# A gated recurrence in twelve sublayers: fills, solve steps and the output step put in another order, output matrices in two buffers

## The chip, the core and the metric

The kernel runs on one core of a Trainium2 chip. The metric is the device time of one execution in microseconds (us). Before the change it is 2972.5 us, the median of three runs (2965.99 to 2985.49).

## The reference, cut to what matters

Twelve sublayers (cross attention, attention and feed-forward, four times) are added to x one after the other; x is 64 sequences of 32 tokens of 128 numbers. The change touches only the fifth, `L1_attn`, a gated delta rule with two states of 64 x 64 in each of 16 heads:

```python
def step(carry, inp):
    S, R = carry
    q_t, k_t, v_t, a_t, aR_t, b_t, g_t = inp
    kn = k_t / jnp.maximum(jnp.linalg.norm(k_t, axis=-1, keepdims=True), 1e-12)
    pred = jnp.einsum('bhji,bhj->bhi', S, kn)
    r = jnp.clip(v_t - pred, -CLIP, CLIP)
    S = a_t[..., None] * S
    kp = jnp.einsum('bhd,bhde->bhe', kn, S)
    S = S + b_t[..., None, None] * kn[..., None] * (v_t - kp)[..., None, :]
    o = jnp.einsum('bhji,bhj->bhi', S, q_t)
    R = aR_t[..., None] * R
    kpR = jnp.einsum('bhd,bhde->bhe', kn, R)
    R = R + g_t[..., None, None] * kn[..., None] * (r - kpR)[..., None, :]
    o = o + jnp.einsum('bhji,bhj->bhi', R, q_t)
    return ((S, R), o)
out = jnp.moveaxis(os, 0, 1).reshape(Bs, Ts, DI) @ Wo.T   # x + out
```

## The kernel before, in words

The sublayer (`l1_attn`) never steps through time. It takes 128 tokens (four sequences) at a time, in 16 groups. For a group it builds, by halving the 32 steps in five levels, the 32 x 32 matrices that say how much of each earlier step reaches each later one, inverts two of them, and applies matrices to the values. All orders are written out by hand, one list for each engine, and the engines wait for each other by counting semaphores. The lists are loops over i from 0 to 17; in round i three groups are in work: group i has its matrices built ("now"), group i-1 is inverted on GpSimd ("mid"), group i-2 is solved and put out ("old"), and group i+1 has its projections made ("new").

TensorE (`@block.tensor`). `fill_s(i, lv)` and `fill_r(i, lv)` compute the products of keys with weighted rows for levels 1 to 4 of the S and the R state (helper `fill`, L3176; 64 small matmuls each, which the trace has as 128 matmul records, since an f32 matmul is two). `fill_0` is level 0 for both states at once, in two halves j, each behind `row0` of its half. `project_q`, `_k`, `_ar`, `_a` are projections of the next group (L3113), `project_nb` and `broadcast` make the key norms (L3149 to L3152, L3164). The old group goes through `values`, then the solve steps y, z, u, p, y2, z2, wr (all in `apply`, L3213, 64 records each), then `step_o` (L3281, L3282, 128 records) and `step_out` (L3295). A solve step needs the step before it, copied out of PSUM by ScalarE or corrected by VectorE.

VectorE (`@block.vector`). `keep_s` and `keep_r` copy the wanted corners of a fill from PSUM into `ms`, `mr`, `ll` under a mask; `advance_s` and `advance_r` multiply the rows, key columns and running gates for the next level, and wait for the fill of their own level, whose operands they overwrite. `corner` (after z and z2) and `clip` (after p) belong to the old group, `turn` and `turn_back` transpose for GpSimd, `norms` and `keys` belong to the next group's keys, `begin` (two halves, twelve instructions, L3398 to L3400) makes the rows for level 0, and `result` adds a finished group to X.

ScalarE (`@block.scalar`). `take` copies a step's result out of PSUM, `take_gate` applies the sigmoids, `widen(i, j)` spreads the five scaled matrices of a group into `wideM` (L3035; j = 1 and 2 are the output matrices), `widen_x` the inverses into `wideX`, `columns` copies the keys. `widen` waits for `scaled`, which GpSimd's `scale(i)` (L2952 to L2956) counts at the end of a group's inversion, and for the step that read the buffer last.

Each list is strict: what stands behind a wait waits too. The end of a round is, on TensorE, wr, `step_o`, `fill_0` of the next group; on VectorE `keep_r(i, 4)`, `begin(i + 1)`, and then `keep_s(i + 1, 0)`, which waits for both halves of `fill_0`.

## Time and profile before

| | us |
|---|---|
| median of three runs | 2972.5 |
| lowest, highest | 2965.99, 2985.49 |
| the profiled execution | 2988.48 |
| its span | 2986.7 |
| TensorE busy in the span | 2402.1 (80%) |
| VectorE busy | 1942.5 (65%) |
| ScalarE busy | 1362.3 (46%) |
| GpSimd busy | 1001.1 (34%) |
| mean granted TensorE clock | 0.89 of full speed |

The numbers are of one profiled execution, which took 16 us more than the median. The recurrence lies between about 880 us and 1946 us of the span, a third of it. The busy shares are averages over twelve sublayers with different limits, so what the change is worth can only be read inside that stretch. "issue" in a wait means that the profile shows nothing that the engine waited for. DMA figures in that stretch are small: no data is loaded there.

### The profile page before, as it was taken

Reading aid. Unit: us, or ns where it says so; the run is one execution under the profiler, and the core shown is the slowest. Engines: PE = TensorE matmul, PEld = TensorE weight load, DVE = VectorE, ACT = ScalarE, POOL = GpSimd, SP = SyncE. Lnnn points to the kernel's source line nnn. Section 1 sums busy time; section 2 is a strip of 40 time slices with the busy share of each in tenths; the row PEclk is TensorE's granted clock in tenths of the full one; section 3 lists DMA queues with packets and bytes.
Section 4 is the critical chain, followed back from the end, with each engine's and each line's share of the span. In section 5 each row is a group of like instructions: output and inputs, shape, how many; then the busy total and the mean of one; then the engine's idle time right before and its main releaser. Section 6 shows DMA issues by size and latency. Waiting matters only on the chain. (4 is left out here: it accounts for less than half of the span.)

```text
span 2986.7 us, 115635 instructions
## 1 busy us (share of the span) xinstructions
PE 2402.1 (80%) x49947; PEld 1863.7 (62%) x49947; DVE 1942.5 (65%) x4625; ACT 1362.3 (46%) x3252; POOL 1001.1 (34%) x1250
## 2 busy tenths in 40 slices
PE   8987478999986688787787886669998997787754
PEld 6755465665555577677776775547776564575633
DVE  3448335777756887777887887257777666564752
ACT  5443133444434344454444543447776553563420
POOL 0000324655550355334553355311111440360004
PEclk9979687999997798998999999969999998897875
DMA  3200331111110000000000000002221003242014
GB/s 101 64 1 29 105 125 53 47 47 46 47 58 2 3 4 4 4 4 4 4 4 4 4 4 4 3 26 62 61 61 61 4 4 108 62 111 67 5 43 122
DMA packets 80270, 117.47 MB, mean 39 GB/s; under 512 B 11490, under 2 KB 66034, under 8 KB 79234
## 3 DMA queue, kind: packets, MB, share of 16 engines
q1 hardware_dynamic: 71250, 100.31, 10.9%
q0 software_dynamic: 8576, 10.53, 1.7%
q8 instruction: 365, 5.98, 0.8%
q14 instruction: 79, 0.65, 0.1%
HBM read 98.16 MB, written 16.51 MB: 38 GB/s over the span
## 5 line engine op out<-in xcount | busy, mean ns | idle before, releaser
L2469 POOL TENSOR_SCALAR l1xs_p<-l1xs_p,l1xs_col 128x257 f32<-128x257 f32 x256 | 234.4, 936 | 204.5 <-DVE l1xs_col L2425 204.5
L3176 PE MATMUL psum<-l1d_rw,l1d_cols 64*32 64x48 f32 x16384 | 191.0, 211 | 111.9 <-issue 86.4
L3176 PEld LDWEIGHTS psum<-l1d_rw,l1d_cols 64*32 64x32 f32 x16384 | 166.3, 109 | 131.3 <-issue 122.6
L2390 ACT ACTIVATE l1xs_p<-psum,l1xs_col 128x257 f32<-128x257 f32 x256 | 119.7, 473 | 209.7 <-DVE l1xs_col L2420 203.6
L2945 POOL TENSOR_TENSOR l1d_kc<-l1d_ms,l1d_beta 128x512 f32<-128x512 f32 x16 | 17.3, 1083 | 493.4 <-DVE l1d_ms L3487 478.1
L3432 DVE TENSOR_TENSOR l1d_rw<-l1d_rw,l1d_tots 128x1536 f32<-128x1536 f32 (+1 forms) x96 | 138.1, 1438 | 65.7 <-PE psum L3176 64.7
L2432 DVE STREAM_TRANSPOSE l1xs_pt<-l1xs_p 128x288 f32<-128x288 f32 x256 | 122.4, 478 | 79.2 <-POOL l1xs_p L2469 79.1
L2977 ACT COPY l1d_ya<-psum 128x512 f32<-128x512 f32 x96 | 54.9, 583 | 222.7 <-PE psum L3213 222.6
L3113 PE MATMUL psum<-XN,l1d_wp 128*128 128x128 f32 x1024 | 143.9, 297 | 10.3 <-issue 8.3
L3113 PEld LDWEIGHTS psum<-XN,l1d_wp 128*128 128x128 f32 x1024 | 131.1, 207 | 23.9 <-issue 20.9
L2354 PE MATMUL psum<-l1xs_pt,l1xs_vals 32*128 32x512 f32 x1152 | 136.6, 604 | 0.0
L2342 PE MATMUL psum<-l1xs_keys,l1xs_qx 128*32 128x257 f32 x2048 | 132.9, 392 | 3.7 <-DVE l1xs_qx L2414 1.9
L2634 PE MATMUL psum<-consts,l2x_p 128*86 128x128 f32 x768 | 118.5, 277 | 0.8 <-ACT l2x_pt L2693 0.5
L1986 POOL TENSOR_TENSOR l2a_phi<-l2a_pos,l2a_ex 128x512 f32<-128x512 f32 x64 | 80.0, 1272 | 116.3 <-ACT l2a_ex L1972 116.3
L2719 ACT ACTIVATE l2x_p<-psum,l2x_top 128x257 f32<-128x257 f32 x256 | 117.9, 475 | 0.2 <-DVE l2x_top L2757 0.2
L2580 POOL TENSOR_TENSOR l2x_lane<-l2x_rec,l2x_pick 128x128 f32<-128x128 f32 x64 | 25.7, 401 | 234.6 <-DVE l2x_rec L2764 129.9
L3213 PE MATMUL psum<-l1d_ya,l1d_wideX 64*64 64x64 f32 x2048 | 89.3, 256 | 17.9 <-issue 10.5
L2420 DVE TENSOR_REDUCE l1xs_col<-psum 128x1 f32<-128x257 f32 x256 | 101.0, 408 | 2.9 <-PE psum L2342 2.6
L2693 DVE COPY l2x_pt<-psum 86x384 f32<-86x384 f32 x128 | 70.8, 553 | 46.5 <-PE psum L2634 36.8
L3213 PEld LDWEIGHTS psum<-l1d_ya,l1d_wideX 64*64 64x64 f32 x2048 | 83.2, 169 | 23.8 <-issue 14.4
L3213 PE MATMUL psum<-l1d_ya,l1d_wideM 64*64 64x64 f32 x2048 | 74.7, 230 | 28.4 <-ACT l1d_a L3007 13.1
L2323 PEld LDWEIGHTS psum<-XN,l1x_wqk 128*128 128x128 f32 x512 | 66.7, 204 | 47.0 <-issue 32.6
(563 smaller groups left out, 6775.9 us busy)
## 6 DMA issues: line engine op xcount, KB each, us to landing
l2f_w<-in_l2f_w SPq DMA_DIRECT2D x16, 768.0 KB
l1xs_vals<-in_ctx_strips SPq DMA_DIRECT2D x16, 576.0 KB
l0f_w<-in_l0f_w SPq DMA_DIRECT2D x15, 579.0 KB
l0x_ctxT<-in_ctxT SPq DMA_DIRECT2D x16, 516.0 KB, 3.8
l1xs_keys<-in_ctxT SPq DMA_DIRECT2D x16, 516.0 KB
l2x_ctxK<-in_ctxT SPq DMA_DIRECT2D x64, 129.0 KB, 2.1
l2x_ctxV<-in_ctxT SPq DMA_DIRECT2D x64, 129.0 KB, 2.1
l3f_w<-in_l3f_w SPq DMA_DIRECT2D x15, 193.5 KB
```

The costliest lines, as they stand in the source:

```text
L2342: mm = nc.tensor.matmul(score_ps(t)[32 * c:32 * c + 32, :S2], qx[:, g % 2, n, 32 * c:32 * c + 32], keys[:, g % 2, c, :S2], start=True, sto ...
L2354: mm = nc.tensor.matmul(u_ps[c][:], vals[r, g % 2, j, :], pt[r, g % 2, :, j, :], start=(j == 0), stop=(j == STRIP - 1))
L2390: nc.scalar.activation(p[:, t % 4, :S2], score_ps(t)[:, :S2], ACT.Exp, bias=col[:, 0, t % 4:t % 4 + 1], accum_out=col[:, 1, t % 4:t % 4 + ...
L2420: nc.vector.tensor_reduce(col[:, 0, t % 4:t % 4 + 1], score_ps(t)[:, :S2], AX.X, ALU.max, negate=True).then_inc(s["mx"], 1)
L2432: nc.vector.transpose(pt[:, g % 2, n].rearrange("p j r -> p (j r)"), p[:, t % 4, :]).then_inc(s["pt"], 1)
L2469: nc.gpsimd.tensor_scalar(p[:, t % 4, :S2], p[:, t % 4, :S2], col[:, 2, t % 4:t % 4 + 1], None, ALU.mult).then_inc(s["norm"], 1)
L2634: mm = nc.tensor.transpose(t_ps[j % 2][:KC, c * 128:(c + 1) * 128], p[:, l, j, c * KC:(c + 1) * KC], k.const("ident"))
L2719: nc.scalar.activation(p[:, l % 2, j, :S2], s_ps[j][:, :S2], ACT.Exp, bias=top[:, l % 2, j:j + 1], accum_out=sums[:, l % 2, j:j + 1]).then ...
L3113: mm = nc.tensor.matmul(k.ps[into + j][:, e * 128:(e + 1) * 128], wp[:, n, c:c + 128], tokens(i), start=True, stop=True)
L3176: mm = nc.tensor.matmul(k.ps[bank0 + pr + e // per * 2][b * T:b * T + T, e % per * w:(e % per + 1) * w], columns[rr, at:at + T], moving[rr ...
L3213: mm = nc.tensor.matmul(k.ps[bank(name) + h // 8][rr, (h % 8) * 64:(h % 8 + 1) * 64], lhs(h)[rr], rhs[rr, h * 64:(h + 1) * 64], start=base ...
L3432: tt(x, x, over, ALU.mult)
```

## The change

What it does, part by part:

1. Output matrices in two buffers. `widen` with j = 1 and 2 writes, for odd groups, into a second tile `wideN`, which is the memory of the layer norm's row buffer (cleared by GpSimd once the norm's columns are read). Those two calls then wait for the `step_o` of the group before the last instead of the last one, and `step_o` reads `output(i, j)`.
2. `fill_0` (both halves) stands ahead of `step_o` on TensorE, and `step_out` of a group moves from the end of its round to the start of the next, behind `values`.
3. Fills, projections and solve steps alternate in another order on TensorE: `project_q` comes behind `fill_s(i, 1)`, `fill_r` of each level stands earlier against the solve steps, `broadcast` comes behind `fill_r(i, 4)`.
4. VectorE: `result` behind `advance_s(i, 0)`; the first `corner` behind `keep_r(i, 1)`; `clip` behind `keep_r(i, 2)`; the second `corner` behind `keep_s(i, 4)`; `keep_r(i, 4)` ahead of `turn_back` and `keys`.
5. ScalarE: all four `widen` calls of group i-1 stand ahead of the copy of wr, and the copy of o comes last, behind `columns` and `widen_x`.

No work is added or removed but for one memset.

```diff
+        wideN = norm.bufs[5][:].rearrange("p c j d -> p (c j d)").rearrange("p (n h t) -> p n h t", n=2, h=H)
+        output = lambda i, j: wideM[:, j] if i % 2 == 0 else wideN[:, j - 1]
...
+            pool.wait_ge(norm.s["cols"], NCH)
+            nc.gpsimd.memset(wideN, 0.0).then_inc(s["zero"], 1)
...
-                if i > 0:
-                    act.wait_ge(s[needs], i * 2)
+                ahead = 1 if j in (1, 2) else 0
+                if i > ahead:
+                    act.wait_ge(s[needs], (i - ahead) * 2)
+                to = output(i, j) if ahead else wideM[:, j]
...
-                if old:
-                    take(i - 2, "wr_mm", ya, "A", "wr")
                 if mid:
                     widen(i - 1, 3)
                     widen(i - 1, 0)
-                if old:
-                    take(i - 2, "o_mm", rd, "B", "o")
-                if mid:
                     widen(i - 1, 1)
                     widen(i - 1, 2)
+                if old:
+                    take(i - 2, "wr_mm", ya, "A", "wr")
                 if new:
                     columns(i + 1)
                 if mid:
                     widen_x(i - 1, 0)
+                if old:
+                    take(i - 2, "o_mm", rd, "B", "o")
...
                 if old:
                     step_wr(i - 2)
-                if old:
-                    step_o(i - 2)
                 if new:
                     fill_0(i + 1, 0)
                     fill_0(i + 1, 1)
                 if old:
+                    step_o(i - 2)
+                if i >= NT:
                     step_out(i - 2)
...
-                if old:
-                    clip(i - 2)
-                if now:
                     keep_s(i, 2)
                     advance_r(i, 2)
                     keep_r(i, 2)
+                if old:
+                    clip(i - 2)
...
+                    keep_s(i, 4)
                 if old:
                     corner(i - 2, "z2_mm", rd, "t2")
                 if now:
-                    keep_s(i, 4)
+                    keep_r(i, 4)
+                if mid:
+                    turn_back(i - 1)
                 if new:
                     keys(i + 1)
-                if mid:
-                    turn_back(i - 1)
-                if now:
-                    keep_r(i, 4)
```

**The end of a full round on TensorE.** Before (z2, `fill_s` of level 4, `broadcast`, `fill_r` of level 4, wr, `step_o`, then, after 60 more of its matmuls in turn, `fill_0` and the next round's first steps):

```order
L3213 MATMUL psum<-l1d_ya,l1d_wideM 64x64 x32
L3176 MATMUL psum<-l1d_rw,l1d_cols 32x48 x64
L3164 MATMUL psum<-l1d_small,l1d_hsel 128x128 x8
L3176 MATMUL psum<-l1d_rw,l1d_cols 32x32 x64
L3213 MATMUL psum<-l1d_ya,l1d_wideX 64x64 x32
L3281 MATMUL psum<-l1d_wideM,l1d_u 64x64
L3282 MATMUL psum<-l1d_wideM,l1d_ya 64x64
...
L3176 MATMUL psum<-l1d_rw 32x112 x64
L3295 MATMUL psum<-l1d_rd,l1d_wo 128x128 x8
L3226 MATMUL psum<-l1d_wv,XN 128x512 x2
```

Now (the lines are numbered five higher; an odd group, whose output matrices lie in the norm's buffer):

```order
L3181 MATMUL psum<-l1d_rw,l1d_cols 32x48 x64
L3218 MATMUL psum<-l1d_ya,l1d_wideM 64x64 x32
L3181 MATMUL psum<-l1d_rw,l1d_cols 32x32 x64
L3169 MATMUL psum<-l1d_small,l1d_hsel 128x128 x8
L3218 MATMUL psum<-l1d_ya,l1d_wideX 64x64 x32
L3181 MATMUL psum<-l1d_rw 32x112 x64
L3286 MATMUL psum<-ln_xn,l1d_u 64x64
L3287 MATMUL psum<-ln_xn,l1d_ya 64x64
```

`fill_0` has passed `step_o`, and `fill_r` of level 4 has passed the broadcasts.

**The end of a full round on VectorE.** Before (second `corner`, `keep_s` of level 4, `keys`, `turn_back`, `keep_r` of level 4, the first instruction of `begin`):

```order
L3534 TENSOR_TENSOR l1d_ya<-psum,l1d_rd 128x512 x2
L3493 COPY_PREDICATED l1d_ll<-l1d_lmask,psum 128x256
L3494 COPY_PREDICATED l1d_ms<-l1d_lmask,psum 128x16x16
L3495 COPY_PREDICATED l1d_ms<-l1d_lmask,psum 128x16x16
L3385 TENSOR_TENSOR l1d_rw<-psum,l1d_cols 128x512 x2
L3528 STREAM_TRANSPOSE l1d_kc<-l1d_xi 128x1024
L3514 COPY_PREDICATED l1d_mr<-l1d_lmask,psum 128x16x16
L3515 COPY_PREDICATED l1d_ll<-l1d_lmask,psum 128x256
L3398 TENSOR_TENSOR l1d_rw<-l1d_rw,l1d_a 128x512
```

Now (the lines are numbered seven higher):

```order
L3500 COPY_PREDICATED l1d_ll<-l1d_lmask,psum 128x256
L3501 COPY_PREDICATED l1d_ms<-l1d_lmask,psum 128x16x16
L3502 COPY_PREDICATED l1d_ms<-l1d_lmask,psum 128x16x16
L3541 TENSOR_TENSOR l1d_ya<-psum,l1d_rd 128x512 x2
L3521 COPY_PREDICATED l1d_mr<-l1d_lmask,psum 128x16x16
L3522 COPY_PREDICATED l1d_ll<-l1d_lmask,psum 128x256
L3535 STREAM_TRANSPOSE l1d_kc<-l1d_xi 128x1024
L3392 TENSOR_TENSOR l1d_rw<-psum,l1d_cols 128x512 x2
L3405 TENSOR_TENSOR l1d_rw<-l1d_rw,l1d_a 128x512
```

The transpose back and the two multiplications of `keys` now stand between `keep_r` of level 4 and `begin`.

**The end of a full round on ScalarE.** Before (the copy of wr, `widen` 3 and 0, the copy of o, `widen` 1 and 2, `columns`, `widen_x`, the copy of the next values):

```order
L2977 COPY l1d_ya<-psum 128x512 x2
L3035 ACTIVATE l1d_wideM<-l1d_ll,l1d_part 128x16x16 x2
L3035 ACTIVATE l1d_wideM<-l1d_ms,l1d_part 128x16x32 x2
L2977 COPY l1d_rd<-psum 128x512 x2
L3035 ACTIVATE l1d_wideM<-l1d_ms,l1d_part 128x16x32 x2
L3035 ACTIVATE l1d_wideM<-l1d_mr,l1d_part 128x16x32 x2
L3052 COPY l1d_cols<-l1d_rw 128x1024
L3055 COPY l1d_cols<-l1d_rw 128x1024
L3045 ACTIVATE l1d_wideX<-l1d_kc,l1d_part 128x16x32 x2
L2977 COPY l1d_v<-psum 128x512 x2
```

Now (an even group; `widen` 0 and 1 show as one row):

```order
L3041 ACTIVATE l1d_wideM<-l1d_ll,l1d_part 128x16x16 x2
L3041 ACTIVATE l1d_wideM<-l1d_ms,l1d_part 128x16x32 x4
L3041 ACTIVATE l1d_wideM<-l1d_mr,l1d_part 128x16x32 x2
L2981 COPY l1d_ya<-psum 128x512 x2
L3058 COPY l1d_cols<-l1d_rw 128x1024
L3061 COPY l1d_cols<-l1d_rw 128x1024
L3051 ACTIVATE l1d_wideX<-l1d_kc,l1d_part 128x16x32 x2
L2981 COPY l1d_rd<-psum 128x512 x2
L2981 COPY l1d_v<-psum 128x512 x2
```

The copy of wr, for which `step_o` waits, now stands behind four `widen` calls that wait for GpSimd.

## Rows read from the trace of the kernel before

**Rows 1.** The page, costliest groups: TensorE's fills, busy, mean ns, idle before.

```profile
L3176 PE MATMUL psum<-l1d_rw,l1d_cols 64*32 64x48 f32 x16384 | 191.0, 211 | 111.9 <-issue 86.4
```

**Rows 2.** The timeline of VectorE: start, duration; first keep of rounds 2 and 15.

```profile
1028.51 1.32 DVE L3465 COPY_PREDICATED l1d_ms<-l1d_imask,psum 128x128 f32<-128x128 int32 x4 [1.91 <-PE psum L3176]
...
1821.48 1.32 DVE L3465 COPY_PREDICATED l1d_ms<-l1d_imask,psum 128x128 f32<-128x128 int32 x4 [4.89 <-PE psum L3176]
```

**Rows 3.** Waits, 1148 to 1822 us, 11 rounds: total, times, longest.

```profile
DVE l1d_ms L3465 <- PE psum L3176: 57.4, 12, 6.0
...
PE psum L3176 <- DVE l1d_tots L3437: 10.9, 11, 1.2
PE psum L3213 <- ACT l1d_a L3007: 10.7, 9, 1.7
```

**Rows 4.** The timeline of TensorE in round 15, a stretch full of fills.

```profile
1852.51 1.41 PE L3176 MATMUL psum<-l1d_rw,l1d_cols 64*32 64x48 f32 x127 [0.93 <-issue]
1856.09 1.32 PE L3176 MATMUL psum<-l1d_rw,l1d_cols 64*32 64x32 f32 x124 [2.17 <-issue]
```

**Rows 5.** Windows there: length, engines' busy us, TensorE clock, DMA share, GB/s.

```profile
1849.60:1850.00 0.40, 0.40 (x22) 0.40 (x18) 0.40 (x1) 0.00 (x0) 0.40 (x1) 1.00 0.19 41
...
1853.60:1854.00 0.40, 0.31 (x28) 0.20 (x15) 0.13 (x1) 0.00 (x0) 0.40 (x1) 1.00 0.17 41
```

**Rows 6.** The timeline of TensorE, start of round 8 and the wr before it.

```profile
1387.56 3.68 PE L3213 MATMUL psum<-l1d_ya,l1d_wideX 64*64 64x64 f32 x64
...
1397.73 2.05 PE L3295 MATMUL psum<-l1d_rd,l1d_wo 128*128 128x128 f32 x16
1399.62 1.88 PE L3226 MATMUL psum<-l1d_wv,XN 128*128 128x512 f32 x4
1401.68 2.02 PE L3113 MATMUL psum<-XN,l1d_wp 128*128 128x128 f32 x16 [0.18 <-DVE X L3548]
1404.48 2.08 PE L3213 MATMUL psum<-l1d_v,l1d_wideX 64*64 64x64 f32 x64 [0.78 <-ACT l1d_v L2977]
```

**Rows 7.** The timeline of VectorE, end of round 7: keys, transpose, keep, begin.

```profile
1384.51 1.29 DVE L3385 TENSOR_TENSOR l1d_rw<-psum,l1d_cols 128x512 f32<-128x512 f32 x2 [2.48 <-PE psum L3164]
1385.84 1.25 DVE L3528 STREAM_TRANSPOSE l1d_kc<-l1d_xi 128x1024 f32<-128x1024 f32 x1
1387.70 0.44 DVE L3514 COPY_PREDICATED l1d_mr<-l1d_lmask,psum 128x256 f32<-128x256 int32 x1 [0.62 <-PE psum L3176]
...
1393.13 0.42 DVE L3400 TENSOR_TENSOR l1d_rw<-l1d_rw,l1d_ar 128x256 f32<-128x256 f32 x1
...
1398.15 1.33 DVE L3465 COPY_PREDICATED l1d_ms<-l1d_imask,psum 128x128 f32<-128x128 int32 x4 [4.61 <-PE psum L3176]
1401.22 0.31 DVE L3548 TENSOR_TENSOR X<-X,psum 128x128 f32<-128x128 f32 x1
```

**Rows 8.** The timeline of VectorE, end of round 0, which has no output step.

```profile
966.47 0.44 DVE L3514 COPY_PREDICATED l1d_mr<-l1d_lmask,psum 128x256 f32<-128x256 int32 x1 [0.38 <-PE psum L3176]
...
974.22 1.30 DVE L3465 COPY_PREDICATED l1d_ms<-l1d_imask,psum 128x128 f32<-128x128 int32 x4 [1.91 <-PE psum L3176]
```

**Rows 9.** Timelines in round 8: TensorE's broadcasts, and VectorE's clip of one half.

```profile
1443.95 1.16 PE L3164 MATMUL psum<-l1d_small,l1d_hsel 32*128 32x128 f32 x16
...
1424.20 0.69 DVE L3542 TENSOR_TENSOR l1d_rd<-psum,l1d_v 128x512 f32<-128x512 f32 x1 [0.21 <-PE psum L3213]
1424.92 0.43 DVE L3543 TENSOR_SCALAR l1d_rd<-l1d_rd 128x512 f32<-128x512 f32 x1
```

**Rows 10.** The timeline of ScalarE and GpSimd near the end of the sublayer.

```profile
1909.24 0.59 ACT L2977 COPY l1d_ya<-psum 128x512 f32<-128x512 f32 x1 [4.21 <-PE psum L3213]
1910.66 0.91 ACT L3035 ACTIVATE l1d_wideM<-l1d_ll,l1d_part 128x256 f32<-128x256 f32 x2
1911.47 1.32 ACT L3035 ACTIVATE l1d_wideM<-l1d_ms,l1d_part 128x512 f32<-128x512 f32 x2
...
1908.96 1.04 POOL L2956 TENSOR_TENSOR l1d_mr<-l1d_mr,l1d_beta 128x512 f32<-128x512 f32 x1
```

42 lines of the change are left out of this document (22 added, 20 removed).

## The prediction

> **What bounds the kernel now.** The page first: its costliest groups name the fills of the recurrence, where most of TensorE's idle time is not a wait for any engine but "issue" [rows 1]. The timeline of VectorE gives the length of a round there: from the first keep of round 2 to that of round 15 are 792.97 us, 13 rounds of 61.0 us [rows 2]. Only these full rounds, with an old, a middle and a new group, are much touched by the change; nothing outside the sublayer is. Then the waits: VectorE waits for the two halves of `fill_0` at the head of every round, 57.4 us in twelve waits, 4.8 us each, while TensorE's waits for other engines are about 1 us a round apiece (for the first `advance_s`, and for the sigmoids ahead of z2) [rows 3].
>
> What is "issue"? In a stretch full of fills the timeline shows stalls 3.58 us apart, 127 matmul records between them, whatever the step at hand [rows 4]. A record has a weight load beside it, so with the waits that is 256 instructions. The windows show the DMA engines at 41 GB/s for 0.4 us, 4.0 us apart, and no data is loaded there: that is 16 KB of instructions each time [rows 5]. So TensorE's instructions arrive in pages, and a new one each 3.6 to 4.0 us, call it 3.7. I count a round from the code: nine times 128 records of fills, seven solve steps of 64, 128 in `step_o`, 64 in the projections and 56 in the rest, 1848, that is 14.6 pages or 54 us of the 61. A page of fills takes 1.4 us and waits 2.2; where few records take long, the instructions wait instead. A round is therefore held by three things in turn: the pages, the chain through fills and VectorE, and TensorE's own order at the end of a round.
>
> The Trainium skill, "Runtime: NRT & Kernel Launch", section "Instruction fetch mechanics", has the same 16 KiB blocks, but says that TensorE holds 128 KiB of them and that a boundary is "mostly hidden". The trace disagrees: 2.17 us were lost at one boundary [rows 4]. By that rule no reordering could win or lose anything at pages; the sum below would stand, and the lower end of its page term would be void.
>
> **The end of a round.** I start at `keep_r(i, 4)`. Before, it and `begin` take 5.85 us to 1393.55, then VectorE waits 4.8 us, because TensorE still does wr (3.68 us at half speed), the copy, `step_o`, and only then `fill_0` [rows 7, 3, 6]: 10.6 us in the mean. Now `fill_0` passes `step_o`, but the transpose (1.25) and `keys` (1.29) have come between [rows 7]. What `fill_0` then costs can be read off round 0, which has no old group: from `keep_r` to the next keep 7.75 us, 1.9 behind the end of `begin` [rows 8]. So 5.85 + 1.25 + 1.29 + 1.9 = 10.3, a gain of only **0.3**. Four of the five microseconds won by passing `step_o` are spent on work that stood in the shadow of fills and now stands in the open, and on a fill at half clock, since TensorE idles in front of it. At full clock (2.08 for 3.68 in a solve step, [rows 6]) the fill's second half would take 1.1, the gain 1.1. A page boundary in the broadcasts, for which `keys` waits, would add up to 2.2 and turn it into a loss of 1.9.
>
> **The rest of a round,** up to `keep_r(i, 4)`:
> - `result` behind `advance_s(i, 0)`: the first fill may start 0.31 us sooner [rows 7]: **-0.3**, at least where TensorE is there in time.
> - `broadcast` behind `fill_r(i, 4)`: that fill comes 1.16 sooner [rows 9]: **-1.2**. Where pages decide, it is 16 records, an eighth of a page, -0.5.
> - `clip` behind `advance_r(i, 2)` and `keep_r(i, 2)`: `project_nb` waits for it, and y2, the next fill and the sigmoids stand behind. `clip` is twice 0.69 + 0.43, 2.2 us [rows 9], which no longer run while TensorE does `fill_r(i, 2)`. It costs 0 where TensorE is late through pages and 2.2 where it is not; but `fill_s(i, 3)`, some 1.4 us [rows 4], now stands ahead of `project_nb` and covers part: **+1.2**, between the two and nearer what is left uncovered.
> - After `fill_0` at half clock, `step_o`, `values`, `step_out` and y have to be done before the first fill. At the solve step's full rate that is at most 2 x 2.08 + 1.88 + 2.05 + 2.08 = 10.2 us; before, `step_out`, `values`, a projection and y were through 8.8 us after 1397.73, just as VectorE was ready [rows 6]. Half speed adds up to 1.6 to a solve step [rows 6]. Bounds 0 and +2; I take **+0.3**, since the two engines have slack again until the second level.
> - Pages: before, `step_out`, `values` and `project_q` stand together, 2.05 + 1.88 + 2.02 us for 36 records [rows 6], and the pages wait. Now the projection is two fills away. Where pages decide the round this is worth up to 2.0; I take **0**, because what ends a round is now the chain of VectorE, which the pages reach only through the fills. Bounds -2.0 and 0.
> - The second buffer for the output matrices, and the first `corner` behind `keep_r(i, 1)`: nothing. `widen` of 1 and 2 no longer waits for `step_o`, but ScalarE idles for long stretches anyway; u waits some 2 us longer for its corner, and its only follower in the chain, p, comes ahead of a `clip` that is itself later. `turn` keeps its place among the fills, so GpSimd's inversion, which ends after `turn` by the same distance, is not later. The memset of `wideN` on GpSimd lies in the prologue, under the projections.
>
> Sum of a round: -0.3 - 1.2 + 1.2 + 0.3 - 0.3 = **-0.3 us**, in 13 rounds **-4**. The ends: low (-0.3 - 1.2 + 0 + 0 - 2.0 - 1.1) = -4.6, high (0 - 0.5 + 2.2 + 2 + 1.9) = +5.6; neither is likely in every round, since a page boundary falls elsewhere each time.
>
> **The last rounds** lose. With no fills left, wr, its copy and `step_o` are the path. The copy of wr began at 1909.24; GpSimd's scale ended at 1910.00 [rows 10]. Now four `widen` pairs stand ahead of the copy, 0.8 for the narrow and 1.25 for each of three others as they follow each other [rows 10], 4.6 us from 1910.0; the copies of wr end at 1915.7 instead of 1910.8. The copy of o, behind `widen_x`, then starts with the end of `step_o`, and all behind it comes some 4.5 us later. In the round before the same order costs about 1, since its scale was done earlier. Together **+5.5**.
>
> The sum is -4 + 5.5 = +1.5 against the profiled execution's 2988.5, so 2990; that execution lies 16 us above the median of its runs, so I forecast **2974 us**, no change. A measurement of this kernel tells about 1%, 30 us, from no change; its three runs alone span 19.5.
>
> **The rivals.**
> - *Pages decide (F).* If the rounds are held by pages rather than by VectorE, the light projection among fills gives its 2.0, the broadcasts 0.5, the first fill 0.3, and VectorE's chain at the end has time to spare with `fill_0` at full clock, 0.8 + 0.3: -3.9 less about 1 for the clock at the head and a part of `clip`, so -2.9 a round, -38 + 5.5: **2940**. For it: 54 of 61 us. Against: a round before already ends with a wait of VectorE that has no page in it.
> - *The exposed chain (S), slower.* `keys` waits for the broadcasts, and `begin` for `keys`, and TensorE for `begin`: three engines' steps in series that nothing covers, ahead of a fill at half clock. If `clip` costs its full 2.2 (+1.0 on my sum), the head the 1.6 of one step at half speed (+1.3), and one round in four loses 2.2 at the broadcasts (+0.5), a round is 2.5 longer: +33 + 5.5, **3011**. It decides as soon as VectorE's idle time at the keep falls under 2 us while the one for `norms` or the broadcasts grows above 2. For it: round 0, where nothing hides the 1.9 us behind `begin` [rows 8]. Against: the pages give TensorE time at each idle.
>
> By the rule on fetching cited above, F would be void and its chance would go to the forecast and to S.
>
> **Chances.** Forecast 0.66 (own range 2955 to 2998), F 0.20, S 0.14. Of F nearly all is faster by over 1% (under 2943) or at its edge, and a little of the forecast's case; of S most is over 3002. So faster 0.19, same 0.69, slower 0.12. The range goes from 2938, with F's value in it, to 3000.
>
> **What would show each step.** VectorE's idle before the first keep at 2 us in place of 4.8, with 10.3 us from `keep_r(i, 4)` to the keep; `fill_0` in two pieces with a gap, the clock at half there; `keep_r(i, 4)` some 50 us behind the first keep, as now (61.0 - 10.6 = 50.4); "issue" still 7 to 9 us a round; in the last rounds `widen` ahead of the copy of wr and 5 us more. Wrong would be a round under 59.5 (F) or over 62.5 (S), or a `widen` wait in full rounds that holds `step_o`.

## The result, and the profile after

The changed kernel takes **3030.9 us** (median of four, 3024.61 to 3059.54) against 2972.5: a ratio of **1.021**, 95% interval 1.0136 to 1.0283, so slower by about 2%. The profiled execution of it took 3024.61 us with a span of 3022.8. It is the fastest of its four, and the profiled execution of the kernel before, 2988.48, was slower than all of its timed runs, so the two profiles differ by 36 us and the medians by 58. What is read from them below explains the 36; the other 22 are not in these two traces.

VectorE's timeline gives the rounds, first keep of round 2 and of round 15, as in [rows 2]:

```profile
1028.31 1.32 DVE L3472 COPY_PREDICATED l1d_ms<-l1d_imask,psum 128x128 f32<-128x128 int32 x4 [1.91 <-PE psum L3181]
...
1854.89 1.32 DVE L3472 COPY_PREDICATED l1d_ms<-l1d_imask,psum 128x128 f32<-128x128 int32 x4 [1.91 <-PE psum L3181]
```

Everything before round 2 is as it was. Thirteen rounds take 826.58 us, **63.58 each**, in place of 61.00: +33.6 us. The last rounds (first keep of round 15 to the end of the last `step_out`) take 132.8 in place of 124.4: +8.4. The rest of the program, behind the last `step_out`, gives 5.7 back: the span grew by 36.1.

I cut each round at the first copy of `keep_r(i, 4)`: the **head** runs from the round's first keep to it, the **end** from it to the next first keep. Means of rounds 2 to 14: head 50.5 before and 53.2 after, end 10.5 before and 10.4 after. So the end of the round does what was forecast, and the head does not.

The fills' group of the page, which answers to [rows 1]:

```profile
L3181 PE MATMUL psum<-l1d_rw,l1d_cols 64*32 64x48 f32 x16384 | 187.4, 208 | 93.3 <-issue 68.1
```

TensorE's "issue" at the fills fell, by 18 us in the whole kernel, while the rounds grew. Its named waits grew instead. The waits of 1148 to 1855 us (total, times, longest), beside [rows 3]:

```profile
PE psum L3181 <- DVE l1d_rw L3407: 31.1, 24, 2.8
DVE l1d_small L3382 <- ACT l1d_small L3024: 23.8, 11, 3.6
DVE l1d_ms L3472 <- PE psum L3181: 19.9, 12, 2.3
PE psum L3154 <- DVE l1d_rd L3550: 15.5, 6, 4.8
PE psum L3118 <- ACT l1d_u L2981: 8.5, 11, 0.8
```

The first keep waits 1.7 us a time in place of 4.8: `fill_0` has passed `step_o`. But TensorE now stands before `fill_0` for VectorE's `begin` (first row), VectorE stands before `norms` for ScalarE's root of the key norms, 2.2 us a round (second), TensorE stands before `project_nb` for the clip (fourth), and before `project_ar` for ScalarE's copy of u (fifth). Before, the wait for the clip was 3.4 us in five times, and those for the root and for u were not there.

The end of round 9 on VectorE and TensorE: `keep_r`, transpose, `keys`, the last of `begin`, first keep; and `fill_0` in two pieces at half clock, as in [rows 7, 8]:

```profile
1460.12 0.44 DVE L3521 COPY_PREDICATED l1d_mr<-l1d_lmask,psum 128x256 f32<-128x256 int32 x1 [1.46 <-PE psum L3181]
...
1460.79 1.24 DVE L3535 STREAM_TRANSPOSE l1d_kc<-l1d_xi 128x1024 f32<-128x1024 f32 x1
1461.95 1.25 DVE L3392 TENSOR_TENSOR l1d_rw<-psum,l1d_cols 128x512 f32<-128x512 f32 x2
...
1468.00 0.42 DVE L3407 TENSOR_TENSOR l1d_rw<-l1d_rw,l1d_ar 128x256 f32<-128x256 f32 x1
1470.33 1.03 DVE L3472 COPY_PREDICATED l1d_ms<-l1d_imask,psum 128x128 f32<-128x128 int32 x3 [1.91 <-PE psum L3181]
```

```profile
1466.02 1.75 PE L3181 MATMUL psum<-l1d_rw 64*32 64x112 f32 x64 [2.14 <-DVE l1d_rw L3407]
1468.47 1.75 PE L3181 MATMUL psum<-l1d_rw 64*32 64x112 f32 x64 [0.71 <-DVE l1d_rw L3407]
```

That is 10.2 us. One window over the thirteen rounds, before and then after (length; busy us and instructions of TensorE, its weight loads, VectorE, ScalarE, GpSimd; TensorE's granted clock, DMA share, GB/s):

```profile
1028.00:1822.00 794.00, 634.21 (x24033) 572.88 (x24015) 632.92 (x1028) 376.94 (x741) 361.14 (x507) 0.93 0.02 4
```

```profile
1028.00:1855.00 827.00, 657.25 (x23901) 593.42 (x23894) 660.07 (x1027) 380.01 (x742) 362.20 (x507) 0.89 0.02 4
```

With the same instructions (but for one `step_o`, which now falls behind the end of the window) TensorE is busy 23 us longer, at a granted clock of 0.89 in place of 0.93 (the mean of stretches at 2.4 and at 1.2 GHz), and **VectorE is busy 27 us longer**. For VectorE the rows by form say which instructions (before, then after):

```profile
L3543 DVE TENSOR_SCALAR l1d_rd<-l1d_rd 128x512 f32<-128x512 f32 x26 | 13.4, 516 | 0.9
...
L3440 DVE TENSOR_TENSOR l1d_tots<-l1d_tots 128x256 f32<-128x256 f32 x26 | 11.1, 426 | 0.9
```

```profile
L3550 DVE TENSOR_SCALAR l1d_rd<-l1d_rd 128x512 f32<-128x512 f32 x26 | 21.6, 830 | 0.9
...
L3447 DVE TENSOR_TENSOR l1d_tots<-l1d_tots 128x256 f32<-128x256 f32 x26 | 20.6, 792 | 0.9
```

The clip's bound took 516 ns in the mean and takes 830; the product of the running gates took 426 and takes 792. Both read and write SBUF only. What they meet there, in round 5, VectorE and then GpSimd:

```profile
1236.02 1.18 DVE L3447 TENSOR_TENSOR l1d_tots<-l1d_tots 128x256 f32<-128x256 f32 x1
...
1250.18 0.43 DVE L3550 TENSOR_SCALAR l1d_rd<-l1d_rd 128x512 f32<-128x512 f32 x1
1250.52 0.68 DVE L3549 TENSOR_TENSOR l1d_rd<-psum,l1d_v 128x512 f32<-128x512 f32 x1
1251.24 1.01 DVE L3550 TENSOR_SCALAR l1d_rd<-l1d_rd 128x512 f32<-128x512 f32 x1
```

```profile
1235.87 1.10 POOL L2949 TENSOR_TENSOR l1d_kc<-l1d_ms,l1d_beta 128x512 f32<-128x512 f32 x1 [29.80 <-ACT l1d_wideX L3051]
...
1250.30 3.29 POOL L2925 TENSOR_TENSOR l1d_tmp<-l1d_lt,l1d_xi 128x512 f32<-128x512 f32 x2
```

The same clip instruction takes 0.43 us when it starts 0.12 us ahead of GpSimd's long one and 1.01 when it starts beside it, while the subtraction from PSUM between them keeps its 0.68. The Trainium skill, "SBUF — State Buffer", section "Who interferes with whom", says that one pair of SBUF ports is shared between VectorE and GpSimd and locked, the loser waiting for it. These rows agree.

In round 16, which has no fills any more, ScalarE's four `widen` calls stand ahead of the copy of wr, as forecast [rows 10]:

```profile
1946.48 0.91 ACT L3041 ACTIVATE l1d_wideM<-l1d_ll,l1d_part 128x256 f32<-128x256 f32 x2 [6.70 <-POOL l1d_mr L2960]
1947.29 1.32 ACT L3041 ACTIVATE l1d_wideM<-l1d_ms,l1d_part 128x512 f32<-128x512 f32 x2
1948.52 1.32 ACT L3041 ACTIVATE ln_xn<-l1d_ms,l1d_part 128x512 f32<-128x512 f32 x2
1949.74 1.32 ACT L3041 ACTIVATE ln_xn<-l1d_mr,l1d_part 128x512 f32<-128x512 f32 x2
1950.96 1.04 ACT L2981 COPY l1d_ya<-psum 128x512 f32<-128x512 f32 x2
```

Counted from round 15's first keep the copies end at 97.1 us in place of 89.3. 4.5 of the 7.8 are the `widen` calls. Another 3.0 were there before them: GpSimd's scale ended 91.6 us behind that keep in place of 88.5. The cause is the same order one round earlier, in round 15, which has no new group. There the four `widen` calls waited for GpSimd, the copy of wr behind them, and `step_o` for the copy:

```profile
1903.53 0.91 ACT L3041 ACTIVATE l1d_wideM<-l1d_ll,l1d_part 128x256 f32<-128x256 f32 x2 [14.55 <-POOL l1d_mr L2960]
...
1909.20 0.44 PE L3286 MATMUL psum<-ln_xn,l1d_u 64*64 64x64 f32 x2 [7.03 <-ACT l1d_ya L2981]
```

Before, `step_o` waited 0.78 us there. All behind it came 3 us later, ScalarE's second `widen_x` too, and GpSimd could begin the next inversion only behind that. In the full rounds, where a new group's fills are at hand, the `widen` calls waited for GpSimd as well (13.8 us in six of them), but no wait of `step_o` shows.

### The profile page after: what moved, and what is told of

Its sections match the earlier page's. It is cut to its first block and busy times, and to the rows that moved or that the text cites. A ratio compares the mean times of both kernels' runs of the same rounds, so it can differ in the third digit from the quotient of the medians.

```text
span 3022.8 us, 115597 instructions
## 1 busy us (share of the span) xinstructions
PE 2421.3 (80%) x49925; PEld 1886.7 (62%) x49947; DVE 1967.2 (65%) x4625; ACT 1364.0 (45%) x3252; POOL 1004.7 (33%) x1251
## 3 DMA queue, kind: packets, MB, share of 16 engines
q1 hardware_dynamic: 71250, 100.31, 10.6%
## 5 line engine op out<-in xcount | busy, mean ns | idle before, releaser
L3439 DVE TENSOR_TENSOR l1d_rw<-l1d_rw,l1d_tots 128x1536 f32<-128x1536 f32 (+1 forms) x96 | 137.3, 1430 | 51.2 <-PE psum L3181 50.8
L2342 PE MATMUL psum<-l1xs_keys,l1xs_qx 128*32 128x257 f32 x2048 | 132.8, 392 | 3.5 <-DVE l1xs_qx L2414 1.9
L2693 DVE COPY l2x_pt<-psum 86x384 f32<-86x384 f32 x128 | 70.8, 553 | 49.4 <-PE psum L2634 36.7
L3218 PE MATMUL psum<-l1d_ya,l1d_wideX 64*64 64x64 f32 x2048 | 83.3, 246 | 19.3 <-DVE l1d_ya L3541 13.8
L2342 PEld LDWEIGHTS psum<-l1xs_keys,l1xs_qx 128*32 128x32 f32 x2048 | 61.7, 111 | 53.6 <-issue 24.4
L2354 PEld LDWEIGHTS psum<-l1xs_pt,l1xs_vals 32*128 32x128 f32 x1152 | 54.5, 184 | 62.7 <-issue 62.5
```

What stands on the lines that cost most here:

```text
L2342: mm = nc.tensor.matmul(score_ps(t)[32 * c:32 * c + 32, :S2], qx[:, g % 2, n, 32 * c:32 * c + 32], keys[:, g % 2, c, :S2], start=True, sto ...
L2354: mm = nc.tensor.matmul(u_ps[c][:], vals[r, g % 2, j, :], pt[r, g % 2, :, j, :], start=(j == 0), stop=(j == STRIP - 1))
L3218: mm = nc.tensor.matmul(k.ps[bank(name) + h // 8][rr, (h % 8) * 64:(h % 8 + 1) * 64], lhs(h)[rr], rhs[rr, h * 64:(h + 1) * 64], start=base ...
L3439: tt(x, x, over, ALU.mult)
```

## The experiments

Each ran in one group with runs of the kernel before on the same chip; times are medians, ratios are to the kernel before of that group, with 95% intervals. Round, head, end and last rounds are read from the profiled execution as above, in us. The kernel before had medians of 2972.5 to 2985.2 in the different groups, so a difference of medians between two groups is good to about 10 us, and the ratios are the safer comparison.

| kernel | time | ratio | round | head | end | last |
|---|---|---|---|---|---|---|
| before | 2972.5 | 1 | 61.00 | 50.5 | 10.5 | 124.4 |
| changed | 3030.9 | 1.021 | 63.58 | 53.2 | 10.4 | 132.8 |
| e1 middle alone | 3048.5 | 1.0207 (1.0165 to 1.025) | 65.98 | 56.3 | 9.7 | 124.2 |
| e2 middle put back | 2993.4 | 1.0048 (1.0023 to 1.0073) | 60.70 | 53.4 | 7.3 | 133.3 |
| e3 norms later | 3032.9 | 1.0165 (1.0122 to 1.0207) | 63.46 | 53.0 | 10.5 | 134.9 |
| e4 ScalarE's last rounds | 3030.8 | 1.015 (1.0106 to 1.0193) | 64.34 | 53.9 | 10.4 | 123.1 |
| e5 fewer records | 2940.6 | 0.9838 (0.9791 to 0.9886) | 57.04 | 49.5 | 7.6 | 123.2 |
| e6 less work | 2980.5 | 0.9979 (0.9957 to 1.0) | 60.53 | 49.4 | 11.1 | 126.8 |
| e7 first half back | 3047.6 | 1.021 (1.0158 to 1.0263) | 64.25 | 53.8 | 10.5 | 134.0 |
| e8 second half back | 3011.6 | 1.0103 (1.0057 to 1.0149) | 61.06 | 50.7 | 10.4 | 135.8 |
| e9 queries back too | 2998.9 | 1.0063 (1.0041 to 1.0086) | 61.85 | 54.5 | 7.4 | 132.5 |
| e10 copy of y first | 2962.6 | 0.9956 (0.9935 to 0.9977) | 58.43 | 51.1 | 7.3 | 132.4 |
| e11 e9 and e4 | 2988.2 | 1.003 (1.0012 to 1.0049) | 61.12 | 53.9 | 7.3 | 126.8 |
| e12 e10 and e4 | 2953.1 | **0.9917** (0.9893 to 0.9941) | 58.61 | 51.4 | 7.3 | 126.6 |
| e13 broadcast back | 3052.9 | 1.0251 (1.0222 to 1.0279) | 65.05 | 54.8 | 10.2 | 134.3 |
| e14 clip back | 3014.7 | 1.0103 (1.0072 to 1.0135) | 62.22 | 51.8 | 10.4 | 134.9 |
| e15 levels 3, 4 back | 3055.5 | 1.0274 (1.0239 to 1.0309) | 63.71 | 53.3 | 10.4 | 135.6 |
| e16 end lists into e10 | 3001.4 | 1.0059 (1.0036 to 1.0082) | 60.31 | 50.1 | 10.2 | 135.3 |
| e17 end lists back | 3029.5 | 1.013 (1.0094 to 1.0167) | 63.62 | 56.1 | 7.5 | 138.1 |
| e18 short GpSimd | 3003.8 | 1.0077 (1.0048 to 1.0106) | 61.55 | 51.2 | 10.4 | 120.0 |

### Which part of the change: e1 and e2

e1 is the kernel before with the round's middle alone in the new order: all moves on TensorE between y and `fill_r(i, 4)`, and those of `corner` and `clip` on VectorE. e2 is the changed kernel with that middle put back, and with the end of the round on VectorE (`keys`, `turn_back`) and the broadcast put back as well:

```diff
+                    fill_s(i, 3)
+                if new:
+                    project_nb(i + 1)
...
+                if old:
+                    clip(i - 2)
```

> The kernel before with the middle of a round alone in the new order (TensorE: fill_r ahead of project_k, z, u, p, project_nb as in the change; VectorE: both corners and clip moved back); the end of the round, the first fill behind step_o and ScalarE's list stay as before. Theory M (the loss is made in the middle: u, p and so clip come late, project_nb waits for clip, norms for project_nb): the stretch from the first keep to keep_r of level 4 grows from 50.4 to about 53 us, the end stays 10.6, so a round of 63.5 to 64 and 33 to 40 us more than before, about 3008. Rival T (the loss comes from the ends: transpose and keys exposed, the clock at half at the head of a round): the middle alone changes nothing, 2972 within 10.

> The change with the middle of a round put back: TensorE's order from project_k to fill_r of level 4 as before, corner and clip and the last keeps, keys and transposes of VectorE as before; the first fill stays ahead of step_o, output matrices in two buffers, step_out at the head of the next round, project_q behind the first fill, ScalarE's new list. Theory M: the end falls to 0.8 + 5.05 + 1.9 = 7.8 us since keys and the transpose are under fills again, the stretch before it stays near 50.4 to 51.5; a round of 58.2 to 59.3, so 22 to 36 us less in 13 rounds, 8 given back in the last rounds: 2945 to 2958. Rival T: no better than the kernel before, 2972 or more, since the head of a round runs at half clock and pages are late. Rival F (pages hold the round): 2972 less 5 at most.

The middle alone costs 5.0 us a round, more than was expected, and 2% of the kernel, as much as the whole change; with it put back the round is 2.9 us shorter, a little more than the 2.6 that the change had cost, but 1.4 to 2.5 longer than was expected of e2. VectorE's wait for the root of the norms is in e1 about what it is in the changed kernel (1157 to 1820 us), and it is missing in e2, e8, e10, e14 and e16, which have the clip at its old place:

```profile
DVE l1d_small L3373 <- ACT l1d_small L3020: 24.6, 10, 4.2
```

The end of a round of e2, 7.3 us, shows what passing `step_o` is worth when nothing else is put there.

### Is the wait for norms to be had back, and the last rounds: e3 and e4

```diff
-                if new:
-                    norms(i + 1)
                 if now:
                     advance_r(i, 3)
                     keep_r(i, 3)
+                if new:
+                    norms(i + 1)
```

> The change with one move on VectorE: norms stands behind advance_r and keep_r of level 3 in place of ahead of them. Theory M: VectorE waited 23.8 us in 11 rounds for the norms that project_nb, late behind clip, feeds; 2.2 us a round. Behind the keep this wait is covered, the round gets 1.5 to 2.2 shorter, 20 to 29 us less than the change: 3003 to 3011. Rival: the wait only moves on (the broadcasts are needed 6 us later all the same, and fill_r of level 3 is late itself): within 8 us of the change, 3023 to 3031.

No gain. The wait at `norms` is gone, but VectorE's wait for fills at `advance` is 76.6 us in place of 37.4 (1157 to 1820 us). So the loss is not a mere matter of where `norms` stands in VectorE's list. e4 is the changed kernel with, on ScalarE, the copy of wr ahead of `widen` 3 and the copy of o ahead of `widen` 1, only where there is no next group:

```diff
+                if old and not new:
+                    take(i - 2, "wr_mm", ya, "A", "wr")
                 if mid:
                     widen(i - 1, 3)
```

> The change with ScalarE's list of before in the last rounds alone (where no new group follows): the copy of wr ahead of the widening, the copy of o between the widenings. The last rounds took 132.9 us from the first keep of round 15 to the end of the last step_out, against 124.5 before. Theory: all of the 8.4 is the copies of wr and o behind the widening: back to 125, the time 8 us less than the change's, about 3023. Rival: only the 5.5 of the forecast come back and 3 stay, which come from the middle of round 15: 3025.

The last rounds fell by 9.7 us, more than the 8.4 that they had lost, and GpSimd's scale in them ended at 87.9 us in place of 91.6, which bears out the cause given above. What the kernel gained is not settled: its median is the changed kernel's, its ratio 1.015 for 1.021, inside both intervals, and its full rounds came out 0.76 us longer in the profile, with ScalarE's list there the same. In e11 against e9 and e12 against e10, where the same edit was made, the medians fell by 10.7 and 9.5 us and the last rounds by 5.8.

### Records or work: e5 and e6

e5 leaves out seven of eight heads in the fourth fill of the output matrices; e6 leaves out three of four blocks in the two gate projections.

```diff
-                fill(cols[:, 2], 5, 7, lv, 2, 32, 8).then_inc(s["mR_mm"], 1)
+                fill(cols[:, 2], 5, 7, lv, 2, 32, 8, range(1 if lv == 4 else hp)).then_inc(s["mR_mm"], 1)
```

> The kernel before, with the fourth fill of the output matrices doing one of its eight heads: it leaves out 112 of a round's 1848 TensorE records and 1.05 us of its busy time, and nothing else, so its output is not the reference's. Two theories of what TensorE's unnamed stalls cost. Theory instructions: a round's length goes with the number of records, since a stall comes every 256 of them. The round falls by more than the work, by about 3.2 us (112 of 1848 records of 61.0 us, 3.7), and the kernel by about 50 us, to some 2925. Rival work: the round falls by the busy time alone, about 1 us, and the kernel by about 16 us, to some 2960. Third, chain: the fourth fill of the output matrices is not on the path of a round (step_out of the block stands behind the next round's start), and nothing changes within 5 us.

```diff
-                    for e in range(4):
+                    for e in range(1 if i > 0 and n >= 2 else 4):
```

> The kernel before, with the projections of the keys' and of the values' correction (project_a and project_ar) doing one of their four blocks a half: it leaves out 24 records and 3.0 us of TensorE's busy time a round, and its output is not the reference's. Theory instructions: the round falls by what 24 records are worth, about 0.7 us, and the kernel by about 12 us, to some 2965. Rival work: the head of a round is bound by TensorE's own busy time, the round falls by nearly all of it, about 3 us, and the kernel by about 45 us, to some 2930. The two kernels together tell whether a round of the kernel before is counted in records or in busy time.

e5: 112 records, 1.05 us of work, and the round is 3.96 us shorter. e6: 24 records, 3.0 us of work, and the round is 0.47 us shorter. So a round follows its records more than its work, as [rows 4] had it. Neither number is the price of records alone. In e5 the granted clock of the rounds was 0.95 in place of 0.93 and TensorE's busy time fell by 1.8 us a round and not by 1.05, so some 0.75 us are faster matmuls; wr alone took 2.9 us in the mean in place of 3.5. In e6 the clock was 0.89, and the busy time fell by 11 us and not by 39, so that what it left out was partly given back by slower matmuls. e5 shows one thing more: 3.0 of its 3.96 us lie in the end of the round, 7.6 us with `step_o` still ahead of `fill_0`. So the end was long in the kernel before at least in part because TensorE came to it late.

### Which half of the middle: e7, e8, e14, e15, e13

e7 puts back the first half in the changed kernel (of VectorE's list the first `corner` alone moves, not the clip), e8 the second.

```diff
                 if old:
                     step_u(i - 2)
+                if now:
+                    fill_s(i, 2)
                 if new:
                     project_ar(i + 1)
```

> The changed kernel with the first half of the round's middle put back (TensorE: fill_r 1 behind z, fill_s 2 behind u; VectorE: corner and clip of level 1 ahead of advance_r 1), the second half left as changed. Theory spread: the 2.9 us a round that putting back the whole middle gave (63.6 to 60.7) comes from both halves alike, and the round comes to about 62, the kernel to about 3010. Rival first: the wait of project_ar for ScalarE's copy of u is most of it, and the round comes to about 61, the kernel to about 2997. Rival second: the half behind it, with the correction's projection and the clip, is most of it, and the round stays at 63.5 with the kernel at 3030.

```diff
+                if old:
+                    step_p(i - 2)
                 if now:
                     fill_r(i, 2)
-                if old:
-                    step_p(i - 2)
...
-                if now:
-                    fill_s(i, 3)
                 if new:
                     project_nb(i + 1)
```

> The changed kernel with the second half of the round's middle put back (TensorE: project_p ahead of fill_r 2, the next block's projection ahead of fill_s 3, the fills of levels 3 and 4 in the old turn; VectorE: clip ahead of keep_s 2, the second corner ahead of keep_s 4), the first half left as changed. Theory spread: about 62 us a round, the kernel at about 3010. Rival first: the round stays near 63.5 and the kernel at 3030, since the first half is what costs. Rival second: the round comes to about 61 and the kernel to about 2997.

The second half is it: 2.5 us a round and 19 us of the kernel; putting back the first half alone gives nothing or costs a little. e14 puts back the turn of `step_p`, `project_nb` and the clip alone, e15 the turn of levels 3 and 4 alone.

> The changed kernel with project_p ahead of fill_r 2, the next block's norms' projection ahead of fill_s 3 and the clip ahead of keep_s 2 on VectorE; levels 3 and 4 as changed. The whole second half gave 2.5 us a round (63.6 to 61.1). Theory clip: TensorE's wait for the clip ahead of project_nb (15.5 us in eleven rounds, 1.4 each) goes and what follows comes earlier, so this half carries most of it: about 61.5 a round, 3000. Rival corner: the levels 3 and 4 carry it, and this run stays within 0.6 us a round of the changed kernel, 3025.

> The changed kernel with levels 3 and 4 put back: the correction's projection ahead of fill_r 3, z2 ahead of fill_s 4, and on VectorE the second corner ahead of keep_s 4; project_p and the clip as changed. Theory clip: at most 0.6 us a round, about 3025. Rival corner: 2 us a round and more, about 61.3, 2998; the wait of z2 for ScalarE's gate (1.6 us, with z2 at half clock behind it, in the kernels with this order) speaks against it.

The clip's part carries 1.4 of the 2.5 us by the profiled rounds. By the ratios it carries all of it, 1.0103 for e14 and for e8; the profiled execution of e14 was its slowest and that of e8 its fastest, so the 1.1 us between their rounds are not safe. Levels 3 and 4 alone give nothing: the kernel got slower by 25 us with them and the profiled rounds by 0.1. Of the 18 us between the two profiled executions 11 lie ahead of round 2 and 3 in the last rounds; why is not shown. e13 puts back only the broadcast ahead of `fill_r(i, 4)`:

```diff
+                if new:
+                    broadcast(i + 1)
                 if now:
                     fill_r(i, 4)
```

> The changed kernel with the broadcast put back ahead of fill_r 4, nothing else. In all kernels with it ahead and step_o behind fill_0 the end of a round took 7.3 us, in those with it behind 10.4. Theory keys: VectorE's product for the keys then comes before keep_r 4 and off the path, the end of a round falls by 3 us and the head grows by the broadcast's 1.2 or a little more, so a round comes to about 61.9 and the kernel to about 3003. Rival trade: the head grows by as much as the end falls (53.2 to 56.2), nothing changes, 3030.

Wrong, and it shows whose the end of the round is: with `keys` still behind `keep_r(i, 4)` on VectorE the end stays at 10.2, though the broadcast comes sooner, and the head pays 1.6 for it.

### The ends: e9, e10, e16, e17

In e2 TensorE stands before the next projection for ScalarE's copy of y (waits of 1157 to 1820 us):

```profile
PE psum L3118 <- ACT l1d_ya L2981: 20.0, 11, 1.8
```

`project_q` had come behind `fill_s(i, 1)`, and on ScalarE the copy of the queries stands ahead of the copy of y. Both next kernels start from e2: e9 puts `project_q` back ahead of y on TensorE; e10 changes ScalarE's list alone.

```diff
                     step_out(i - 3)
+                if new:
+                    project_q(i + 1)
                 if old and i != NT + 1:
                     step_y(i - 2)
```

> The changed kernel with the middle of the round put back and the next block's query projection put back ahead of step_y as well: of TensorE's lists only step_o behind fill_0 and step_out behind the next round's values are left of the change. In the run with the middle put back, TensorE stood 1.81 us a round behind fill_s 1 for ScalarE's copy of y, which had the copy of the queries ahead of it, and 0.72 ahead of fill_s 1. Theory shadow (step_o costs the head, and the head pays for the order of queries and y): the queries' 2.05 us go under VectorE's work ahead of the first fill, fill_s 1 starts about 1.3 us later, and the 1.8 us wait goes, so that a round falls by about 2.5 us, from 60.7 to 58.2, and the kernel from 2993 to about 2955. Rival pages: the time of a round goes with the number of records alone, which is unchanged, and the kernel stays at about 2993 (60.7 a round).

```diff
+                if old:
+                    take(i - 2, "y_mm", ya, "A", "y")
                 if new:
                     take_q(i + 1)
                 if old:
-                    take(i - 2, "y_mm", ya, "A", "y")
                     widen_x(i - 2, 1)
```

> The changed kernel with the middle put back, the query projection left behind fill_s 1 as changed, and on ScalarE the copy of y ahead of the copy of the queries. Theory shadow: the wait of 1.81 us for the copy of y goes, and with no TensorE work moved the round falls by up to 1.8, from 60.7 to about 59, the kernel to about 2967. Rival pages: nothing, about 2993. Where this one gains and the one with the queries ahead of step_y does not, it was ScalarE's queue; where both gain, the wait behind fill_s 1.

e9 missed, 61.85 us a round for 58.2. Its trace has a new wait of 2.1 us a round: the projection of the queries writes the bank that `result` reads, and `result` now stands behind `advance_s(i, 0)` and `step_out`. No run moved `result`, so how much of the miss it is stays open:

```profile
PE psum L3118 <- DVE X L3555: 21.4, 10, 2.9
```

e10 gained 31 us on e2 by the medians, 2.3 us in each round. It has `step_o` behind `fill_0`, the two buffers and what goes with them (`step_out`, `result` and `project_q` later, ScalarE's new list), and it is 0.4% faster than before: the idea of the change is worth 2.6 us a round (61.00 to 58.43) where the lists around it fit. That is by one profile of each; the medians, 16 us apart with 8 us lost in the last rounds, say nearer 2. The end of one of its rounds, `keep_r`, the last of `begin`, first keep, is VectorE's `begin` and half a fill, with nothing between:

```profile
1426.47 0.40 DVE L3521 COPY_PREDICATED l1d_mr<-l1d_lmask,psum 128x256 f32<-128x256 int32 x1
...
1432.46 0.42 DVE L3407 TENSOR_TENSOR l1d_rw<-l1d_rw,l1d_ar 128x256 f32<-128x256 f32 x1
1434.42 1.04 DVE L3472 COPY_PREDICATED l1d_ms<-l1d_imask,psum 128x128 f32<-128x128 int32 x3 [1.54 <-PE psum L3182]
```

e16 puts the change's end of the round into e10 (broadcast behind `fill_r(i, 4)`, `turn_back` and `keys` behind `keep_r(i, 4)`); e17 takes it out of the changed kernel.

```diff
-                if new:
-                    keys(i + 1)
-                if mid:
-                    turn_back(i - 1)
                 if now:
                     keep_r(i, 4)
+                if mid:
+                    turn_back(i - 1)
+                if new:
+                    keys(i + 1)
```

> The kernel that gained on ScalarE's queue, with the changed order at the end of a round put back in: the broadcast behind fill_r 4, and on VectorE turn_back and keys behind keep_r 4. Theory VectorE: the end of a round is VectorE's own row of work from keep_r 4 on (two copies 0.8 us, four passes of begin 5.2 to 5.9, and now the transpose's 1.25 and the keys' 1.29 as well), so it grows from 7.3 to about 10; the head gives back the broadcast's 1.2 us; a round grows by 1.4, from 58.4 to about 59.8, the kernel from 2963 to about 2985. Rival free: the head gives back 2.7 us, and the kernel stays within 6 us.

> The changed kernel with the broadcast ahead of fill_r 4 and keys and turn_back ahead of keep_r 4, as before. Theory VectorE: the end of a round falls from 10.4 to 7.3 us, the head grows by 1.2 to 1.6 as it did where the broadcast alone was put back (53.2 to 54.8), and a round comes to about 62, the kernel to about 3010. Rival free: head and end trade one for one, 63.6 and 3030.

With the old middle these lists cost 1.9 us a round and 39 us (1.0% by the ratios; 7 us of it ahead of round 2 and 3 in the last rounds of the profile); with the new middle nothing. There what the end saves the head takes. Their price depends on the chain ahead of them.

### The two repairs together: e11 and e12

e11 is e9 and e12 is e10, each with e4's edit.

> The kernel with only step_o, step_out and result moved (queries ahead of step_y, middle as before) and with ScalarE's old list in the last two rounds as well. Its rounds are those of the kernel with the queries ahead of step_y; the last round falls by 8 to 10 us, as it did where ScalarE's old list was put into the changed kernel (132.8 to 123.1 from the first keep of round 15 to the end). Theory: about 2946, below both the kernel before and the changed one by 1% and more. Rival: the last rounds give it back in another place, within 4 us of the run without it.

> The kernel that gained on ScalarE's queue (middle put back, copy of y ahead of the copy of the queries), with ScalarE's old list in the last two rounds as well. The rounds are unchanged at 58.4 us and the last one falls by 6 to 10 (132.4 to 126.8 or 123.1, as in the two runs with the old list): about 2955, some 0.8% below the kernel before. Rival: the last rounds give it back, and it stays at 2963.

e12 is the fastest of these kernels that leaves nothing out: 2953.1 us, 0.8% under the kernel before and, by the medians, 2.6% under the changed one. e11 gained its 10.7 us too, but stands on e9's wait.

### GpSimd beside the clip: e18

The changed kernel with GpSimd's long instructions cut short from the second group on, all lists as changed:

```diff
-                            ins = tt(t4[n], left(lb[:, n, hi, lo]), right(xb[:, n, lo, lo]), ALU.mult)
+                            ins = tt(t4[n][:, :few], left(lb[:, n, hi, lo])[:, :few], right(xb[:, n, lo, lo])[:, :few], ALU.mult)
```

> The changed kernel with GpSimd's long instructions cut short from the second group on: the two products of gather on 4 of 16 heads, the two products of merge_last on one of eight rows; the output is not the reference's. Theory contention: VectorE's small instructions beside them fall back to 0.43 us, its busy time by some 1.5 us a round, most of it in the chain through the clip, project_nb and norms, and a round falls by 1 to 2 us, from 63.6 to about 62, the kernel by 16 to 30 us, to about 3008. Rival order: what the new middle costs is the waits in its lists; VectorE's busy time falls and its idle time grows by as much, and the kernel stays within 6 us of 3031.

Its rounds, and the product of the running gates in them:

```profile
1036.00:1836.00 800.00, 643.58 (x23892) 580.55 (x23893) 620.45 (x1027) 377.58 (x741) 279.03 (x507) 0.91 0.02 4
```

```profile
L3448 DVE TENSOR_TENSOR l1d_tots<-l1d_tots 128x256 f32<-128x256 f32 x26 | 12.1, 466 | 0.9
```

792 ns are down to 466, VectorE's busy time falls by 40 us, the round by 2.0 (26 us in thirteen rounds) and the kernel by 27. The last rounds fall by 12.8, where GpSimd's scale ends at 80.4 us in place of 91.6, and round 2 starts 7 us later. The edit takes away more contention than the change added (VectorE is 12 us under its busy time in the kernel before) and shortens GpSimd's chain in the rounds too, so it is no price for the change's part.

Two kernels above hold against a large one. e7 has the product of the running gates back at 426 ns and VectorE's busy time near that of before; e8 has neither. Their windows over the thirteen rounds and that product, e7 and then e8:

```profile
1029.00:1865.00 836.00, 657.75 (x23915) 594.14 (x23901) 636.12 (x1028) 378.87 (x742) 357.83 (x507) 0.90 0.02 4
L3446 DVE TENSOR_TENSOR l1d_tots<-l1d_tots 128x256 f32<-128x256 f32 x26 | 11.1, 426 | 0.9
```

```profile
1030.00:1824.00 794.00, 638.09 (x23895) 577.02 (x23891) 657.20 (x1027) 378.52 (x741) 366.40 (x507) 0.91 0.02 4
L3446 DVE TENSOR_TENSOR l1d_tots<-l1d_tots 128x256 f32<-128x256 f32 x26 | 20.6, 792 | 0.9
```

e7 spares VectorE 24 of the 27 us and its rounds are 0.7 us longer than the changed kernel's; e8 spares it 3 and its rounds are 2.5 shorter. So the contention is real and the order decides the time. It came in two places: at the product with the first half of the middle, and at the clip's bound, 830 ns in the changed kernel and 495 in e8, with the second.

## Why the prediction was wrong, by its own steps

I forecast 2974 with a round 0.3 shorter, the rival "exposed chain" at 3011 with a round 2.5 longer. A round is 2.6 longer and the last rounds are 8.4 longer.

- **The end of a round: right.** 10.3 forecast, 10.4 measured (from 10.6 by my reading of before, 10.5 by this one). What passing `step_o` gives and what `keys` and `turn_back` take back are both in it: 7.3 without them (e10), 10.2 with them (e16).
- **Broadcast behind `fill_r(i, 4)`, -1.2: right in size.** The head rose by 1.6 in e13, which puts back that alone. From e10 to e16 it fell by 1.0, but there `keys` and the transpose left the head too.
- **`step_o` and a slow clock at the head, +0.3: not contradicted.** The head of e10 is 0.6 over that of before, with `step_o` and other moves in it.
- **`clip` behind `keep_r(i, 2)`, +1.2: this step failed.** I let one term stand for the whole middle of the round and set its upper bound, 2.2, by the length of the clip's own four instructions. The middle costs 5.0 us where it is alone (e1), 2.9 between e2 and e17, and 5.2 between e10 and e17, which differ in ScalarE's copy of y too. What the term left out: `step_p` itself had moved behind `fill_r(i, 2)`, so that p starts 3.8 us later after the first keep (28.7 for 24.9, mean of the rounds) and `project_nb` 6.3 (35.7 for 29.4); behind `project_nb` stand ScalarE's root and then `norms` in VectorE's list, which waited 2.2 us a round. The turn of the clip, `step_p` and `project_nb` alone is 1.4 us of it by the profiles (e14). VectorE's small instructions also slid beside GpSimd's long ones, which the forecast had at nothing without a reason; e7 and e8 speak against a large price for that.
- **"The first `corner` behind `keep_r(i, 1)`: nothing", `project_ar`: not priced.** `project_ar` now comes directly behind u and waits for its copy, 0.8 us in each of eleven rounds. Undoing that half alone gave nothing (e7), so it is no large part of the loss.
- **Pages, 0 in the sum:** "issue" did fall, from 9.7 to 6.4 us a round, but TensorE's waits for other engines grew by more, from 2.8 to 6.8. So the rival that made pages decide (F, 2940) was wrong, though e5 agrees that records cost more than their work.
- **`project_q` behind `fill_s(i, 1)`** I took for a move with no cost but pages. It leaves TensorE waiting for the copy of y behind that of the queries on ScalarE, 2.3 us a round in e2 (e10 has them back); in the changed kernel `fill_r(i, 1)` stands between, and that wait is 1.6 us in eleven rounds.
- **The last rounds, +5.5: right in mechanism, 8.4 in size.** The four `widen` calls are 4.5 of it, as worked out. The term for the round before, "about 1", was mis-sized: that round cost 3.0, because `step_o` waited 7.0 us there for the copy of wr, and GpSimd's next inversion began as much later.
- **The exposed chain (S)** had the right sum for a round, 63.5, by luck: it put 0.5 on the broadcasts and 1.3 on the head's clock, which the runs don't show, and the clip's 2.2 was less than the middle cost. Its 3011 is 20 us under the measured median. Its condition was met on both sides: the first keep waits 1.7 us, under 2, and `norms` 2.2, over 2.

What stays open: about 2.5 of the middle's 5 us are found in no single move (e7, e14, e15 apart give 1.4 or less, e2 gives 2.9), and where contention, slower clock and order overlap in them no run here separates. Nor does any trace show where the 22 us are by which the medians differ more than the two profiles.

## What to carry to other kernels

When a step of a hand-written order moves, cost the chain behind it to the engine that waits last, not the step's own length: here the moves around a clip of 2.2 us put p 3.8 us later and the norms' projection 6.3. A change that bundles a good idea with rearrangements should be timed in parts: the step behind the fill was worth some 2 to 2.6 us a round, and the rest lost 5. An order has to be kept alike on both sides of a copy: ScalarE's list had the copy of the queries ahead of the copy that TensorE waited for. Look in a timeline at what GpSimd does at the place where a small SBUF instruction of VectorE is going to land, but don't take VectorE's busy time for the kernel's.
